# Index words loaded in two parts, and filling records with 1024 different indices

## The reference

```
# layer 2
h = silu(nodes @ Wh + bh)
h = propagate(h);  h = several dense layers with residuals;  h = propagate(h)

def propagate(h):
    x_edge = silu(concat(h[src], h[dst], edge_attr) @ We + be)
    x_edge = (edge_attr @ Wl) * x_edge
    return segment_mean(x_edge, src) + h

# layer 3, attention with two heads
alpha = leaky_relu((h[src] * att_i).sum(-1) + ((h[dst] + ee) * att_j).sum(-1))
alpha = softmax of alpha over the edges of one src
out = segment_sum((h[dst] + ee) * alpha, src).mean(heads) + bias
```

## Time and profile before

| | us |
|---|---|
| median of 3 runs | 14575.41 |
| lowest and highest | 14569.86, 14580.77 |
| span of the profiled execution | 14544.7 |
| PE, POOL busy | 9475.1, 9384.7 |
| DVE, ACT busy | 7196.0, 3845.8 |
| layers 0 and 1 end | about 6921 |
| the two passes of layer 2 | 7113 to 9436, 9622 to 11951 |
| the edge pass of layer 3 | 12040 to about 14480 |

### The profile page before, as it was taken

How to read it: one execution, slowest core, us unless ns; L and a number is a source line. 1 busy time by engine, 2 the same in 40 slices (tenths; PEclk the granted TensorE clock), 3 DMA queues, 4 the chain that set the end, 5 groups by cost and what they waited for, 6 DMA issues and landing times.

```text
span 14544.7 us, 196674 instructions
## 1 busy us (share of the span) xinstructions
PE 9475.1 (65%) x40895; PEld 6378.7 (44%) x40896; DVE 7196.0 (49%) x18628; ACT 3845.8 (26%) x8556; POOL 9384.7 (65%) x8465
## 2 busy tenths in 40 slices
PE   0366665776638788788466666676666655666665
PEld 0011122222113333433366666546666655666665
DVE  8877665777720000000233333333343337999996
ACT  0244445444301111111122222222222212333322
POOL 0278887888865445445377777647777756777773
PEclk9999999999968888788555555555555555566655
DMA  9932222222239999899944444524444458888886
GB/s 382 403 53 19 20 18 16 19 21 19 20 85 383 351 354 376 317 357 369 64 104 103 104 104 104 79 65 103 105 104 103 103 70 164 176 175 176 176 174 106
DMA packets 1604026, 2197.52 MB, mean 151 GB/s; under 512 B 1003915, under 2 KB 1046987, under 8 KB 1575629
## 3 DMA queue, kind: packets, MB, share of 16 engines
q1 hardware_dynamic: 1028588, 1491.01, 37.2%
q0 software_dynamic: 453120, 343.50, 15.7%
q10 hardware_dynamic: 121698, 356.43, 6.7%
HBM read 1771.19 MB, written 419.98 MB: 151 GB/s over the span
## 4 chain that ended last, share of the span: by engine, by line
POOL 37%; issue 18%; DMA 16%; PE 15%; DVE 8%; SPq 3%; DVEq 1%; another core or an unknown queue 1%; ACT 1%; POOLq 0%; ACTq 0%
POOL gat L658 23%; POOL adj L628 13%; DMA arena<-adj 10%; PE bank L1043 6%; DMA adj<-put_n,put_at 4%; PE bank L1253 2%; PE same L1262 2%; DVE arena L1370 1%; DMA b_row<-acc 1%; DVE arena L1697 1%; POOL rec_src L614 1%; PE same L1175 1%; PE bank L1262 1%; PE same L1014 1%
## 5 line engine op out<-in xcount | busy, mean ns | idle before, releaser
L658 POOL DMA_INDIRECT gat<-q_table,ring_i x3456 | 3487.4, 1009 | 1512.6 <-issue 1051.6
L628 POOL DMA_INDIRECT adj<-put_n,put_at x1632 | 2557.4, 1567 | 1267.4 <-DVE put_at L1454 638.2
L614 POOL DMA_INDIRECT rec_src<-pay,ring_i x1632 | 1604.4, 983 | 1485.9 <-ACTq L756 1004.2
L1197 PE MATMUL bank<-onehot_t,onehot 128*128 128x64 f32 x6912 | 1584.6, 424 | 1448.0 <-DVE acc L1592 1017.2
L658 POOL DMA_INDIRECT arena<-h_table,ring_i x1728 | 1731.8, 1002 | 744.9 <-issue 513.3
L1197 PEld LDWEIGHTS bank<-onehot_t,onehot 128*128 128x128 f32 x6912 | 1507.1, 330 | 1524.5 <-DVE acc L1592 995.8
L1102 PE MATMUL same<-onehot 32*128 32x512 f16 x3264 | 1678.7, 615 | 621.2 <-DVE onehot L1425 389.6
L1043 PE MATMUL bank<-arena,hs 128*64 128x512 f32 x5880 | 1576.5, 699 | 597.1 <-DMA arena<-adj 595.7
L1187 PE MATMUL bank<-hs,arena 128*128 x6912 | 1564.9, 421 | 160.8 <-ACT arena L880 160.8
L1433 DVE TENSOR_SCALAR_CACHE_REDUCE onehot<-same 128x128 bf16<-128x128 f32 (+3 forms) x1632 | 1233.2, 756 | 842.6 <-PE same L1104 791.9
L1187 PEld LDWEIGHTS bank<-hs,arena 128*128 128x128 f32 x6912 | 1525.7, 333 | 163.2 <-issue 163.2
(11 more groups left out here) (277 smaller groups left out, 12816.7 us busy)
## 6 DMA issues: line engine op xcount, KB each, us to landing
arena<-adj SPq DMA_DIRECT2D x300, 2560.0 KB, 19.8
arena<-rec_src SPq DMA_DIRECT2D x3456, 69.0 KB
adj<-hs ACTq DMA_DIRECT2D x25, 6656.0 KB, 46.3
rec_src<-pay ACTq DMA_DIRECT2D x1, 119232.0 KB, 332.3
arena<-lo_row SPq DMA_DIRECT2D x3456, 32.0 KB
hs<-b_row SPq DMA_DIRECT2D x432, 256.0 KB
acc<-b_row SPq DMA_DIRECT2D x432, 256.0 KB
gat<-q_table,ring_i POOLq DMA_INDIRECT x3456
```

The costliest lines, as they stand in the source:

```text
L614: nc.gpsimd.indirect_dma_start(rec_src, bass.IndirectOffsetOnAxis(ring_i[:, q, u:u + 1], 0), pay[:, q, u, :], None, bounds_check=SLOTS - 1 ...
L628: nc.gpsimd.indirect_dma_start(counts, bass.IndirectOffsetOnAxis(put_at[:, b // 3 % 4, c:c + 1], 0), put_n[:, b // 3 % 4, c:c + 1], None, ...
L658: nc.gpsimd.indirect_dma_start(rows[n][:, u, :], None, table, bass.IndirectOffsetOnAxis(ring_i[:, n, u:u + 1], 0)).then_inc(landed[n], 16)
L1197: last = mm(bank[6 + n % 2][:, u // 2 * D:(u // 2 + 1) * D], onehot[:, n % 2, u, :], msg[n % 2][:, u, :], start=u % 2 == 0, stop=u % 2 == 1)
```

## The change

The fill pattern's index is no longer 0: record u of partition p gets u * 128 + p, so the 8 tiles of a group hold 1024 different indices in their empty slots. The words are loaded in two parts: tiles 0 to 511 (`TA`) by SP into `d_tab[0]`, the other 1216 by ACT into `d_tab[1]`, issued when the first part has landed. PE's and ACT's work for the dense layer and the projection stands ahead of the digit transposes. The first four digit blocks are transposed, copied and stored before SP's first edge loads; the others inside the first pass: PE and ACT after turn `FA` = 8, SP's store and DVE's wait for the second part after turn `FB` = 12. `lo_sb` moves from the arena into `pay`, and the transposes from banks 2 to 5 to banks 0 to 3. The loops of the first pass are split in two at these points.

```
@@ -37,6 +37,8 @@
+TA = 4 * P
+FA, FB = 8, 12
@@ -58,6 +60,7 @@
+assert FA < FB and 4 * U * (FB + 1) <= TA < TT and NG % 4 == 0
@@ -229,6 +231,7 @@
+        lo_sb = pay[:].rearrange("p q u r -> p (q u r)")[:, 0:14 * P // 2].bitcast(BF16).rearrange("p (b e) -> p b e", b=14)
@@ -338,7 +341,7 @@
-        d_tab = sem("d_tab")
+        d_tab = [sem(f"d_tab{n}") for n in range(2)]
@@ -507,7 +510,7 @@
-            sp.dma_start(tabs[1][:, 0:TT, :], rec_src.rearrange("(p t) r -> p t r", p=P)[:, :, 0:RD]).then_inc(d_tab, 16)
+            sp.dma_start(tabs[1][:, 0:TA, :], rec_src.rearrange("(p t) r -> p t r", p=P)[:, 0:TA, 0:RD]).then_inc(d_tab[0], 16)
@@ -515,11 +518,17 @@
-            sp.wait_ge(a_lot, 4)
-            full = TT // P
-            sp.dma_start(lo_row[0:full * P].rearrange("(b t) e -> t b e", t=P), lo_sb[:, 0:full, :]).then_inc(d_lo, 16)
-            sp.dma_start(lo_row[full * P:TT], lo_sb[0:TT - full * P, full, :]).then_inc(d_lo, 16)
-            sp.wait_ge(d_lo, 32)
+            def store_first_digits():
+                sp.wait_ge(a_lot, 1)
+                sp.dma_start(lo_row[0:TA].rearrange("(b t) e -> t b e", t=P), lo_sb[:, 0:TA // P, :]).then_inc(d_lo, 16)
+                sp.wait_ge(d_lo, 16)
+
+            def store_other_digits():
+                full = TT // P
+                sp.wait_ge(a_lot, 4)
+                sp.dma_start(lo_row[TA:full * P].rearrange("(b t) e -> t b e", t=P), lo_sb[:, TA // P:full, :]).then_inc(d_lo, 16)
+                sp.dma_start(lo_row[full * P:TT], lo_sb[0:TT - full * P, full, :]).then_inc(d_lo, 16)
+                sp.wait_ge(d_lo, 48)
@@ -538,15 +547,26 @@
-                with sp.Fori(1, NG // 4) as i:
-                    for n in range(4):
-                        sp.wait_ge(l_msg, i * 4 + (k * NG + n - 3 + OFF))
-                        sp.wait_ge(l_oht, i * 4 + (k * NG + n - 3 + OFF))
-                        load_edges(k, i, n)
-
-            for k in range(2):
-                store_table(EV_PQ + k, q_table[k], acc[:])
-                load_all_edges(k)
+
+                def more(first, end):
+                    with sp.Fori(first, end) as i:
+                        for n in range(4):
+                            sp.wait_ge(l_msg, i * 4 + (k * NG + n - 3 + OFF))
+                            sp.wait_ge(l_oht, i * 4 + (k * NG + n - 3 + OFF))
+                            load_edges(k, i, n)
+
+                if k:
+                    more(1, NG // 4)
+                else:
+                    more(1, FB)
+                    store_other_digits()
+                    more(FB, NG // 4)
+
+            store_table(EV_PQ, q_table[0], acc[:])
+            store_first_digits()
+            load_all_edges(0)
+            store_table(EV_PQ + 1, q_table[1], acc[:])
+            load_all_edges(1)
@@ -850,13 +870,18 @@
             act.wait_ge(s_w, 16 * W_LOADS)
-            for b in range(4):
+            for q in range(2):
+                act.wait_ge(d_scat[q], EI * 16 * U)
+            act.wait_ge(d_tab[0], 16)
+            act.dma_start(tabs[1][:, TA:TT, :], rec_src.rearrange("(p t) r -> p t r", p=P)[:, TA:TT, 0:RD]).then_inc(d_tab[1], 16)
+
+            def digit_rows(b):
                 act.wait_ge(p_lot, b + 1)
                 if b < 3:
-                    act.copy(lo_sb[:, 4 * b:4 * b + 4, :], bank[2 + b][:].rearrange("p (b e) -> p b e", b=4)).then_inc(a_lot, 1)
+                    act.copy(lo_sb[:, 4 * b:4 * b + 4, :], bank[b][:].rearrange("p (b e) -> p b e", b=4)).then_inc(a_lot, 1)
                 else:
-                    act.copy(lo_sb[:, 12, :], bank[5][:, 0:P])
-                    act.copy(lo_sb[0:TT % P, 13, :], bank[5][0:TT % P, P:2 * P]).then_inc(a_lot, 1)
+                    act.copy(lo_sb[:, 12, :], bank[b][:, 0:P])
+                    act.copy(lo_sb[0:TT % P, 13, :], bank[b][0:TT % P, P:2 * P]).then_inc(a_lot, 1)
             for c, (c0_, n) in enumerate(CHUNKS):
@@ -894,13 +919,24 @@
-                with act.Fori(0, NG // 4 - 1) as i:
-                    for n in range(4):
-                        group(i, n)
+
+                def groups(first, end):
+                    with act.Fori(first, end) as i:
+                        for n in range(4):
+                            group(i, n)
+
+                if k:
+                    groups(0, NG // 4 - 1)
+                else:
+                    groups(0, FA)
+                    for b in range(1, 4):
+                        digit_rows(b)
+                    groups(FA, NG // 4 - 1)
...
+            digit_rows(0)
@@ -1155,14 +1191,14 @@
-            pe.wait_ge(d_tab, 16)
-            for b in range(4):
+            def digit_rows(b):
...
-                        last = nc.tensor.transpose(bank[2 + b][0:m, j * P:(j + 1) * P],
+                        last = nc.tensor.transpose(bank[b][0:m, j * P:(j + 1) * P],
...
+
@@ -1199,10 +1235,21 @@
                 look_up(0, 0)
-                with pe.Fori(0, NG // 4 - 1) as i:
-                    for n in range(4):
-                        look_up(i + (n + 1) // 4, (n + 1) % 4)
-                        sums(i, n)
+
+                def groups(first, end):
+                    with pe.Fori(first, end) as i:
+                        for n in range(4):
+                            look_up(i + (n + 1) // 4, (n + 1) % 4)
+                            sums(i, n)
+
+                if k:
+                    groups(0, NG // 4 - 1)
+                else:
+                    groups(0, FA)
+                    pe.wait_ge(d_tab[1], 16)
+                    for b in range(1, 4):
+                        digit_rows(b)
+                    groups(FA, NG // 4 - 1)
                 for n in range(4):
@@ -1214,6 +1261,9 @@
+            pe.wait_ge(n_ev, NCH * (EV_PQ + 1))
+            pe.wait_ge(d_tab[0], 16)
+            digit_rows(0)
@@ -1284,7 +1334,7 @@
-            v.memset(pay[:, :, :, 1], PAD_LO).then_inc(s_fillable, 1)
+            do(v.memset(pay[:, :, :, 1], PAD_LO))
@@ -1292,6 +1342,7 @@
+            v.tensor_scalar(pay[:, 0, :, 0], iota_lo[:, 0:U], float(P), neg_p[:, 0:1], ALU.mult, ALU.subtract).then_inc(s_fillable, 1)
@@ -1533,7 +1584,8 @@
-            dve.wait_ge(d_tab, 16)
+            for q in range(2):
+                dve.wait_ge(d_scat[q], EI * 16 * U)
@@ -1602,15 +1654,25 @@
+                dve.wait_ge(d_tab[0], 16)
...
-                with dve.Fori(1, NG // 4 - 1) as i:
-                    for n in range(4):
-                        group(i, n)
+
+                def groups(first, end):
+                    with dve.Fori(first, end) as i:
+                        for n in range(4):
+                            group(i, n)
+
+                if k:
+                    groups(1, NG // 4 - 1)
+                else:
+                    groups(1, FB)
+                    dve.wait_ge(d_tab[1], 16)
+                    groups(FB, NG // 4 - 1)
```

More of the change, by code:

```diff
@@ L162, in build @@
         lo_bc = [edge[:, o4 + n * U * P // 2:o4 + (n + 1) * U * P // 2].bitcast(BF16) for n in range(4)]
-        lo_sb = edge[:, o4:o4 + 14 * P // 2].bitcast(BF16).rearrange("p (b e) -> p b e", b=14)
         assert o4 + 2 * U * P <= 12 * CE + TT - 2 * NP
```

## The result

The changed kernel takes 14445.42 us (median of 4, 14427.44 to 14447.52), the kernel before beside it on the same chip 14577.01 (median of 4). The ratio is 0.9906, 95% interval 0.9892 to 0.9920: some 132 us less. I had predicted 14358 and a range from 14310; the result lies outside. Both things that the change is for happened at the size I gave them. Something that I had priced at nothing took 100 us back.

A forecast was written before the change was run, and what follows sets the result against it. The prediction took POOL's issuing of row gathers as the bound, with stops at layer 2's door and the pass ends. 95.0 - 3.7 + 126 = 217 us off the span gave 14328, plus 30.7 gave 14358 us; range 14310 to 14430.

The forecast's parts named there:

- (d): Other digits, inside layer 2's first pass: extra transposes, copies, store and waits cost 0; the split loop 0, bound 3 us.
- (a): Door to layer 2: the words' first part lands after 41.4 us, and everything up to the table store moves forward 95.0 us.
- (b): Door to layer 2: the words' second part, 94.4 us alone, runs beside the table store and costs it 3.7 us.
- (c): First digits, before SP's first edge load: group 0's one-hot rows come about 10 us later, covered; cost 0, bound 10 us.
- (e): Fill: one small DVE instruction more and the fill released a few memsets later, cost 0.
- (f): Pass ends: distinct rows bring the last groups to normal pace, gaining 41.3 and 41.3 us in layer 2, 43.5 in layer 3.
- The offset: Whole kernel: the timed median lies 30.7 us above the profiled span, and this was kept for the forecast.
- "Slower": Rival, 4%: in layer 2's first pass the words' second part starves and PE waits for it at group 32; 14668 us.
- "Part B goes first": Rival, 10%: at layer 2's door the table store and all after it wait for the words' second part; gain 169, 14406 us.

The follow-up runs named there:

- a_pad8: The changed kernel with 8 semaphore increments added to DVE's program between the two layer-2 passes: 14315 us, ratio 0.9821.
- b_pad152: The kernel before with 152 semaphore increments added to DVE's program between the two layer-2 passes: 14671 us, ratio 1.0060.
- b_pad160: The kernel before with 160 semaphore increments added to DVE's program between the two layer-2 passes: 14611 us, ratio 1.0010.
- a_idle: The changed kernel with PE also waiting for the second part of the words before the transposes of h: 14506 us, ratio 0.9949.
- a_early: The changed kernel with ACT's copies not behind the word load and SP, not ACT, issuing the words' second part: 14460 us, ratio 0.9922.

## Why the prediction was wrong

The step that failed is in (d): "A split loop adds a loop entry: 0, bound 3 us". I priced the instructions that the split adds where they run, and found none. They cost 100 us where they don't run, in layer 3, by moving another loop. The fault is of kind and not of size, and my range had no room for it. With the loop 8 instructions further (a_pad8) the change takes 0.9821 of the time, which is 14316 beside a kernel before of 14577: inside the range, and 42 us under the forecast.

I could have had it. The earlier trace rows give 10.86 us a step in layer 3, and the waits of before list "DVE hs L1668 <- issue" once a turn: a stop with no releaser behind each backward branch. The Trainium skill, "Runtime: NRT & Kernel Launch", section "Instruction fetch mechanics", says in my words that most engines hold 32 KiB of instructions, 512, refill them in blocks, and stall at a taken branch whose target is outside. DVE's loop has 531. The trace agrees with the kind of it, with 3.2 us a turn before the change. Where it differs the measurement decides: the page has blocks of 16 KiB, the queue's packets here are of 8 KB, one per 128 instructions; and a loop of 365, well under 512, is still fetched anew. It doesn't say that the cost depends on the position; that is what b_pad152 and b_pad160 show, 91.7 against 87.0 us a turn for 8 instructions.

And I would have had to see that DVE has nothing to hide it behind: it is busy for 81 of the 87 us of a turn and waits for no one.

The other steps:
- (a) part A and the order: -95.0 predicted, -95.0 measured; landing 41.2 us (41.4 predicted). That the dense layer's stretch would stay at 42 us was wrong in this execution (+9.1) and right in others of the same order.
- (b) 3.7 us predicted, 3.1 in the ledger and 3.3 by a_idle. Part B alone: 94.4 predicted, 93.6 and 94.2 measured. Beside the store and the loads it took 152.9, not 95 to 110, and no one waited for it.
- (c) The first SiLU comes 30.7 us after POOL's first gather, not 19.1: 12 us later where I had said about 10, and covered, as I had said (the bound there took SP's issues beside the fill as stretched 2.5-fold; the earlier trace rows give 3-fold); POOL waited 1.2 us for indices in 7060:7130.
- (e) nothing, as said.
- (f) 43.1 and 41.7 in layer 2, for 41.3 and 41.3, and 53.1 in layer 3 for 43.5. No POOL wait for an index in 9200:9330.
- The offset. I added the 30.7 us by which the timed median of before lay over its profiled span. That was right for a forecast of the median, and it means that the profiled execution of before was a fast one: in the 15 runs here the median lies between 26 under and 28 over the span. So of the 217 us 132 were measured by the medians, and 103 by the two profiled spans. In which stretch the median execution of before is slower than the profiled one, no trace shows.
- The rivals. "Slower" had no trace of truth (and its time was added up wrong: part B landing 750 us after its issue would start PE's group 32 at 7713 instead of 7374, 339 us late, so 14697 and not 14668). "Part B goes first" didn't happen: issue 0.38 us, first gather 16.7 us on. On SP's queue, a_early, it did.

By the ledger: 217 predicted, less 100 for the loop's place, less 9 and 9 for the clock's scatter, less 5 for the later load, plus 9 for layer 3's tail, gives 103.

## What to carry to other kernels

An edit that only adds instructions still moves every loop behind it: where a loop's body has some hundreds of instructions, look for a wait "for issue" at its first lines and for a steady count of instruction packets a turn, before and after, and price a change of place at some microseconds a turn. Put padding or a hint on it rather than take the place that comes. Then ask who sets the pace: on an engine that waits for no one, as DVE here, every microsecond of standstill lengthens the turn, and 8 us instead of 4 cost 4 a turn. And put a long load on another queue than the short store that comes next.

## What was unexpected

- 8 instructions of padding, nothing else, made the changed kernel 0.85% faster, and 152 made the kernel before 0.6% slower.
- Gathering 1024 different rows instead of one took the packet from 0.72 to 0.061 us in layer 2 and from 0.63 to 0.146 in layer 3.
- The same two stretches of dense layer kept the full clock for less or longer from one execution to the next, which moved the door by 9 us and, with other causes not excluded, the stretch between the passes by up to 29.
